# Dense diffusion stage of a four-layer graph network: the centred features go to TensorE unscaled, the deviation is applied to the product

## The reference

```python
def _layernorm(x, axis=-1, eps=1e-05):
    m = jnp.mean(x, axis=axis, keepdims=True)
    v = jnp.var(x, axis=axis, keepdims=True)
    return (x - m) / jnp.sqrt(v + eps)
...
h = jnp.maximum(_layernorm(x, axis=-1), 0.0)
x = x + _L0_gnn_ref(h, edge_index, L0_gnn_W, L0_gnn_b)
...
h = x @ W.T + b                      # in _L0_gnn_ref
diffusion = ALPHA * (agg - h)        # ALPHA = 0.05
reaction = BETA * jax.nn.relu(h)     # BETA = 1.5
return h + diffusion + reaction
```

## Time and profile before

| | us |
|---|---|
| median of 3 runs | 7889.76 |
| lowest and highest run | 7882.79, 7894.85 |
| the profiled execution | 7882.55 |
| its span, first to last instruction | 7880.5 |
| mean granted TensorE clock over the span | 0.808 |

### The profile page before, as it was taken

How to read it: one execution, slowest core, us unless ns; L and a number is a source line. 1 busy time by engine, 2 the same in 40 slices (tenths; PEclk the granted TensorE clock), 3 DMA queues, 4 the chain that set the end, 5 groups by cost and what they waited for, 6 DMA issues and landing times. The chain is left out here.

```text
span 7880.5 us, 102247 instructions
## 1 busy us (share of the span) xinstructions
PE 4974.4 (63%) x32610; PEld 4394.4 (56%) x32610; DVE 4621.6 (59%) x5713; ACT 1144.6 (15%) x1724; POOL 3952.6 (50%) x3347
## 2 busy tenths in 40 slices
PE   4555334666057787555555885666668775685797
PEld 2354233555057777455554775666657675574675
DVE  6999544111577766566666762322376696584357
ACT  0133111222024300122221000111100142000001
POOL 0288666655067600677774007777700003775765
PEclk9855666777579999766666997777789997898899
DMA  2276566544932255323332553443445686122009
GB/s 71 64 213 205 158 137 126 99 96 86 343 111 73 62 187 189 90 78 81 78 81 66 192 195 101 113 112 106 112 129 194 233 311 225 43 58 97 14 13 261
DMA packets 836386, 1024.65 MB, mean 130 GB/s; under 512 B 587119, under 2 KB 600324, under 8 KB 834892
## 3 DMA queue, kind: packets, MB, share of 16 engines
q1 hardware_dynamic: 501260, 626.23, 26.3%
q10 hardware_dynamic: 190528, 303.71, 10.9%
q0 software_dynamic: 144256, 90.12, 7.8%
HBM read 608.19 MB, written 417.84 MB: 130 GB/s over the span
## 5 line engine op out<-in xcount | busy, mean ns | idle before, releaser
L838 POOL DMA_INDIRECT gc_msgs<-t,src_rows x784 | 755.6, 964 | 1183.3 <-POOLq L146 889.6
L888 POOL DMA_INDIRECT acc<-de_sums,de_put x392 | 680.3, 1735 | 449.6 <-DMA acc<-de_sums,de_put 180.2
L1883 PE MATMUL gc_ring<-gc_msgs,gc_hot 128*128 x4736 | 651.3, 296 | 235.7 <-SPq L1842 234.4
L1883 PEld LDWEIGHTS gc_ring<-gc_msgs,gc_hot 128*128 128x128 f32 x4736 | 624.8, 209 | 311.2 <-issue 303.1
L838 POOL DMA_INDIRECT at1s_ends<-x,src_rows x392 | 389.8, 994 | 578.2 <-POOLq L146 459.0
L838 POOL DMA_INDIRECT at2s_ends<-h,src_rows x392 | 369.9, 944 | 616.7 <-POOLq L146 497.6
L838 POOL DMA_INDIRECT at1s_ends<-x,dst_rows x392 | 419.0, 1069 | 119.5 <-issue 119.5
L838 POOL DMA_INDIRECT re_rows<-x,src_rows x392 | 403.9, 1030 | 133.9 <-issue 124.3
L1017 PE MATMUL de_ps<-de_win,de_pick 128*128 x2368 | 419.9, 351 | 78.0 <-ACT de_pick L1033 45.1
L1017 PEld LDWEIGHTS de_ps<-de_win,de_pick 128*128 128x128 f32 x2368 | 404.6, 262 | 108.8 <-issue 102.1
L1000 PE MATMUL de_ps_pick<-de_near,de_hot 128*128 x1184 | 154.0, 273 | 477.8 <-issue 418.2
(11 more groups left out here) (460 smaller groups left out, 11954.9 us busy)
## 6 DMA issues: line engine op xcount, KB each, us to landing
rew_win<-x SPq DMA_DIRECT2D x74, 544.0 KB, 5.1
at1w_win<-g SPq DMA_DIRECT2D x74, 544.0 KB, 5.0
at2w_win<-g SPq DMA_DIRECT2D x74, 544.0 KB, 5.0
de_win<-t SPq DMA_DIRECT2D x74, 512.0 KB, 4.4
de_near<-same SPq DMA_DIRECT2D x74, 512.0 KB, 5.5
x<-rew_win ACTq DMA_DIRECT2D x74, 512.0 KB, 5.0
h<-at1w_win ACTq DMA_DIRECT2D x74, 512.0 KB, 4.9
h<-at2w_win ACTq DMA_DIRECT2D x74, 512.0 KB, 5.0
```

The lines of the kernel that those rows point to most:

```text
L838: nc.gpsimd.indirect_dma_start(buf[:, t * width:(t + 1) * width], None, table, bass.IndirectOffsetOnAxis(ap=rows[:, t:t + 1], axis=0)).the ...
L888: nc.gpsimd.indirect_dma_start(g.acc0[j % 2], bass.IndirectOffsetOnAxis(ap=put[:, j:j + 1], axis=0), sums[:, j * D:(j + 1) * D], None, com ...
L1883: done = nc.tensor.matmul(ring[:, bass.ds(to[n], SLOT)], hot[k][:, n, :], each_group(msgs[:, bass.ds(of[n], MID)], SLOT // MID), start=Fal ...
```

## The change

The pass that scales `cen` (`scale`, L751) is gone. TensorE transposes `cen` as soon as it is centred. The product in PSUM is multiplied by the reciprocal deviation, spread over each group of 64, into `h0` (L754 of the new kernel), signalled as `grown`; a new pass adds the bias to `h0` in place (L756); the blend stays (L758 there). The reciprocal moves to the head of `close`. TensorE's products wait for `grown` of the chunk two back, not for `h_made`. The lists of VectorE and ScalarE are one step shorter: `close` has distance 2, not 3, and on ScalarE `norm` has 0, `turn` 1, `positive` 2.

```diff
--- before.py
+++ after.py
@@ -707,8 +707,8 @@
         stored = [r.sem(f"stored{k}") for k in range(DEEP)]
         last_in = r.sem("last_in")
         grow = r.sb("grow", [P, COLS])
-        x_free, o_free, link_s, squared, centred, summed, rooted, normed, turned, evac, product, h_made, mixed, relued, scaled, ready, cleared, lo_made, blended = (r.sem(n) for n in (
-            "x_free", "o_free", "link", "squared", "centred", "summed", "rooted", "normed", "turned", "evac", "product", "h_made", "mixed", "relued", "scaled", "ready", "cleared", "lo_made", "blended"))
+        x_free, o_free, link_s, squared, centred, summed, rooted, grown, turned, evac, product, h_made, mixed, relued, scaled, ready, cleared, lo_made, blended = (r.sem(n) for n in (
+            "x_free", "o_free", "link", "squared", "centred", "summed", "rooted", "grown", "turned", "evac", "product", "h_made", "mixed", "relued", "scaled", "ready", "cleared", "lo_made", "blended"))
         with nc.Block() as block:
             @block.sync
             def _(sp):
@@ -744,24 +744,22 @@
                     dve.wait_ge(squared, b.number + 1)
                     nc.vector.tensor_reduce(sd[:, s, :], grouped(sq[s % 2][:, :], D), AXX, ALU.add).then_inc(summed, 1)
 
-                def scale(b):
+                def close(b):
                     s = b.slot
                     dve.wait_ge(rooted, b.number + 1)
                     link(nc.vector.reciprocal(sd[:, s, :], sd[:, s, :]))
-                    nc.vector.tensor_tensor(grouped(cen[s][:, :], D), grouped(cen[s][:, :], D), spread(sd[:, s, :], D), ALU.mult).then_inc(normed, 1)
-
-                def close(b):
-                    s = b.slot
                     dve.wait_ge(product, b.number + 1)
                     dve.wait_ge(scaled, b.number + 1)
                     dve.wait_ge(o_free, b.number + 1)
-                    nc.vector.tensor_tensor(grouped(h0[s % 2][:, :], D), grouped(psH[s % 2][:, :], D), each_group(g.w["b0"][:, :], J), ALU.add).then_inc(h_made, 1)
+                    nc.vector.tensor_tensor(grouped(h0[s % 2][:, :], D), grouped(psH[s % 2][:, :], D), spread(sd[:, s, :], D), ALU.mult).then_inc(grown, 1)
+                    dve.wait_ge(grown, b.number + 1)
+                    nc.vector.tensor_tensor(grouped(h0[s % 2][:, :], D), grouped(h0[s % 2][:, :], D), each_group(g.w["b0"][:, :], J), ALU.add).then_inc(h_made, 1)
                     dve.wait_ge(h_made, b.number + 1)
                     nc.vector.scalar_tensor_tensor(hi[s][:, :], h0[s % 2][:, :], 0.95, x[s][:, :], ALU.mult, ALU.add).then_inc(blended, 1)
 
                 link(nc.vector.reciprocal(grow[:, :], g.dis[:, :]))
                 link(nc.vector.tensor_scalar(grow[:, :], grow[:, :], 20.0, None, ALU.mult))
-                pipeline(dve, order=[(2, scale), (1, variance), (3, close), (0, centre)], slots=DEEP)
+                pipeline(dve, order=[(1, variance), (2, close), (0, centre)], slots=DEEP)
 
             @block.scalar
             def _(act):
@@ -798,16 +796,16 @@
                     act.wait_ge(stored[b.slot], 48 * b.nth)
                     act.sem_inc(o_free, 1)
                 act.sem_inc(o_free, DEEP)
-                pipeline(act, order=[(1, norm), (1, root), (2, turn), (3, positive), (5, store), (6, landed)], slots=DEEP)
+                pipeline(act, order=[(0, norm), (1, root), (1, turn), (2, positive), (4, store), (5, landed)], slots=DEEP)
 
             @block.tensor
             def _(pe):
                 def turn(b):
                     s = b.slot
-                    pe.wait_ge(normed, b.number + 1)
+                    pe.wait_ge(centred, b.number + 1)
                     transpose_pairs(nc, psT[s % 2], cen[s], g.ident, J // 2).then_inc(turned, 1)
                     pe.wait_ge(evac, b.number + 1)
-                    once_past(pe, h_made, b, 2)
+                    once_past(pe, grown, b, 2)
                     times(nc, psH[s % 2], hT[s % 2], g.w["w0"], J // 2).then_inc(product, 1)
                 pipeline(pe, order=[(0, turn), (2, nothing)], slots=DEEP)
```

## The result

| | us |
|---|---|
| before, median of 4 runs | 7887.11 (7882.79 to 7894.85) |
| changed, median of 4 runs | 8061.40 (8058.03 to 8073.88) |
| ratio | 1.0223, 95% interval 1.0205 to 1.024 |
| the profiled execution of the changed kernel | 8061.66, span 8059.7 |

The change makes the kernel 2.2% slower; 8058 was predicted. Nearly all of it comes from the stage. Its last GpSimd pass ended at 812.64 before and ends at 981.52 now, 168.9 later; 168.5 was the sum. The profiled executions differ by 179.1 us, so some 10 us lie elsewhere, within what runs of one kernel spread (16 us here). Half of them come soon behind the stage: the next stage's first GpSimd pass starts 168.9 later (819.53 and 988.40), but the first gather of re_rows 173.9 later (2198.6 and 2372.5). The cause is not known.

The account below looks back on a forecast made before the run. VectorE, 98.6% busy, and its turns with GpSimd were taken as the bound. After the change, 46 chunks at 13.4 us plus start and tail add 168.5 us, giving 8058 against the median; range 8026 to 8096.

Parts of the forecast that it names:

- the sum: Whole stage: chunk times and tail added up put the last GpSimd pass at 981.1 instead of 812.64, +168.5 us.
- The chain: Steady chunks: centring, square, evacuation, products, L754, L756, blend, next centring follow without VectorE overlap; 13.4 us a chunk.
- T: The end of L693, the centring pass, of the newest chunk; times within a chunk count from it.
- The tail behind the last T: End of the stage: remaining VectorE and GpSimd passes of the last two chunks, to +25.2 us.
- The account of a chunk's loss: Per chunk 3.5 us more: 4.7 new idle time and 0.6 holding in L756, less 1.9 holding gone with L751.
- ScalarE's part: ScalarE's square, root, evacuation, relu in strict order: evacuation ends T+2.2 to 2.4, relu T+3.2 to 3.5.
- The holding of L756: New bias pass, SBUF to SBUF, waits for GpSimd's scaling pass and ends 1.08 after it; takes 1.8 us.
- L754 not held: Scaling pass reading PSUM runs beside GpSimd in 1.21 us; the rival, held, had 14.65 a chunk, 8115, chance 0.06.
- Not slower: Rival: evacuation done ahead of the square, product ready by T+2.6, VectorE not idling; 7880 us, chance 0.03.
- the turns: VectorE and GpSimd passes that exclude each other; in the kernel before they nearly fill a chunk's 9.86 us.
- clock near 0.5: Sign in the changed profile: TensorE stays near half clock, with products at 3.8 us.
- the clock rises: Rival: TensorE's products run at full clock in 2.05 us; 12.9 us a chunk, 8035 in all, chance 0.08.

Follow-up runs that it names:

- the PSUM experiment: Changed kernel with ScalarE's square after evacuation and relu, scaling result left in PSUM for the bias pass: 9239.42 us, ratio 0.9975 to the kernel before.
- the first experiment: Changed kernel with only ScalarE's list reordered: root, evacuation and relu ahead of the newest chunk's square; 9260.86 us, ratio 0.999 to the kernel before.
- The bf16 experiment: Changed kernel with the evacuated tile and first layer's weight in bf16, shortening the products: 9418.83 us, ratio 1.0162 to the kernel before.
- the last experiment: Changed kernel run again without edit, beside the kernel before on its experiment chip: 9427.53 us, ratio 1.0172.

## Why the prediction was right

The predicted time was 8058, the measured 8061.4, and the step-by-step sum holds in the steady chunks, which make nearly all of it. That the totals are as near as 3 us is partly luck: the stage gave 168.9 for 168.5, but the medians differ by 174.3, and what lies outside the stage was not forecast.

- *The chain.* The third T came at 339.32, predicted 339.5; then 46 chunks at 13.42, predicted 13.4; the end at 981.52, predicted 981.1. These rows carry it (timeline of the changed kernel, then its end):

```profile
338.10 1.22 DVE L693 TENSOR_TENSOR dd_cen<-dd_x,dd_sums 128x1024 f32<-128x1024 f32 x1
```

```profile
955.23 1.22 DVE L693 TENSOR_TENSOR dd_cen<-dd_x,dd_sums 128x1024 f32<-128x1024 f32 x1
...
979.62 1.90 POOL L828 TENSOR_TENSOR dd_base<-dd_base,dd_grow 128x1024 f32<-128x1024 f32 x1 [0.18 <-POOL dd_base L826]
```

- *The tail behind the last T (956.45).* It was forecast at 25.2 and took 25.1, but its passes came in another order, so the length is right by luck. The last chunk's products ran at the full clock, and L756 of that chunk was through at T+13.5, before L826 of the chunk before it (L828 in the prediction's numbering), where the prediction had L756 end at T+15.8, behind it:

```profile
965.30 2.05 PE L684 MATMUL dd_psH<-w_w,dd_hT 128*128 128x128 f32 x16 [1.11 <-ACT dd_hT L781]
...
968.71 1.22 DVE L756 TENSOR_TENSOR dd_h<-dd_h,b_b 128x1024 f32<-128x1024 f32 x1
```

- *The account of a chunk's loss.* The prediction's 4.7 of new idle time and 0.6 of holding, less 1.9, make 3.4 and not the 3.5 it gives. Measured are 4.7 of idle time (3.53 and 1.13) and 0.5 of holding in L756; the chunk is 3.56 longer than in the earlier trace rows.

- *ScalarE's part.* Evacuation from T+1.19 to T+2.19 (607.82 to 609.01, 610.01), predicted 2.2 to 2.4; relu over at T+3.1, predicted 3.2 to 3.5. Queued activations overlapped by 0.1, as read from the one pair of the earlier trace rows.
- *GpSimd.* L826 followed the relu by 0.45 and not 0.26. I had the distance from a release by GpSimd's own pass; by ScalarE it is longer. By luck it made up for the relu's being early: L826 at T+3.58, predicted 3.5.
- *The holding of L756.* 1.72 in the mean, predicted 1.8; the experiment without the relu add shows that it is GpSimd's turn, and 0.52 a chunk.
- *L754 not held.* 1225 ns, predicted 1.21 us; it ran beside L828 in 47 of 49 chunks, and L828 had its undisturbed 1.90 as well (1915 ns in the mean), so neither held the other. That rival is out, and the PSUM experiment shows the reason: of the bias pass it changes nothing but the place of one input.
- *Not slower.* The rival's condition was made on purpose in the first experiment, and its outcome came as the rival said: the turns set 9.75 us a chunk (the rival had 9.9), and the total is that of the kernel before.
- *VectorE busy* at 64%, predicted 65; the wait in front of L754 3.62.

One statement was off, without effect on the time: "clock near 0.5". The clock did rise, in the wrong place. Windows of the changed kernel (columns as in the first view of the result section):

```profile
610.06:613.80 3.74, 3.74 (x17) 3.74 (x18) 0.26 (x2) 0.90 (x1) 2.35 (x1) 0.50 0.74 294
...
615.60:619.00 3.40, 0.00 (x0) 0.00 (x0) 3.37 (x3) 0.00 (x0) 2.06 (x2) 0.93 0.00 0
...
621.00:623.50 2.50, 0.00 (x0) 0.00 (x0) 1.38 (x2) 2.18 (x4) 0.00 (x0) 0.50 0.97 294
```

The clock is at half speed (0.50, which is 1.2 GHz) through the 3.7 us of products and at 0.93 in the 3.4 us behind products and transposes, when TensorE has nothing left to compute; it is back at 0.50 in the 2.5 us ahead of the next products. The mean of the steady stretch is 0.63. So the rival "the clock rises" came about by half: the engine's clock rose, the products in the steady rows still took 3.4 to 3.8 us. The bf16 experiment bounds what faster products could have given: 2.75 us less product were worth 0.57 us a chunk, 26 us in all; the rival's own figure was 23.

## What to carry to other kernels

When a pass is moved behind a product to take it off the road to TensorE, the pass itself may be free while the order of steps is not. In a kernel whose engines work lists in strict order, go once round the circle from the newest chunk's last step, list by list, and see whether an old chunk's step stands behind a new chunk's; then a shorter pipeline makes the whole circle the time of a chunk, with no engine above 64% busy. If two branches leave the same point and meet again, measure them apart and together: each alone showed a fifth of its length here. And where VectorE and GpSimd share a stage, count the VectorE passes with two SBUF inputs as turns; letting a pass leave its result in PSUM for the next one to read took a turn away and gave the only kernel that is clear of the kernel before on the fast side (ratio 0.9975). These are not all the turns: the small L692 has one input in SBUF and takes 0.17 us in the start of the changed kernel's stage (320.04), but 0.63 at 619.40, to 0.04 behind the end of L820, while the sum L691 beside the same L820 keeps its 1.21. What sets these two apart was not tested.

## What the runs showed of the hardware that I had not expected

The same program, the kernel before, takes 17% longer on the two chips of the experiments (9263.17 and 9265.57 us against 7887.11, medians), while the changed kernel's dense stage is equal to 0.01 us a chunk. The difference shows in stages with gathers by index. The rows are of the products of the graph convolutions' edges in the changed kernel, of the first runs and then of the last experiment (columns: engine, operation, tile, count: shortest/median/longest ns, first and last start in us):

```profile
L1881 PE MATMUL gc_ring<-gc_msgs,gc_hot x4736: 272/276/578, 6828.9 to 7885.9; 128*128 x198
```

```profile
L1881 PE MATMUL gc_ring<-gc_msgs,gc_hot x4736: 269/275/580, 7445.8 to 9252.7; 128*128 x198
```

The matmuls have nearly the same median, 276 and 275 ns, but their stretch lasts 1057 us in one and 1807 us in the other. Other gathers show it too: those of the second attention's source rows (at2s_ends) start over 976 us in one and over 1299 in the other, with a median of 944 ns each in both. The profile puts 302 us of TensorE's idle time in front of those products down to "issue" in one and 1536 in the other, that is, to nothing it can name. What makes the time longer was not tested; it may be the chip, or something else that changed between the first runs and the experiments.
